# Two transformer layers on one core: wide score passes, narrower maxima, and normalisations, splits and last quantisation steps on GpSimd

## The reference

```python
xn = layernorm(x)
# layer 0, attention A, 16 heads of 8: cosine scores
W = (1 - arccos(clip(l2norm(q) @ l2norm(k).T, -0.999, 0.999)) / pi) ** 16
attn = (W / (W.sum() + eps)) @ v @ Wo.T + bo
# layer 0, "ffn": softmax attention (16 heads of 8) + 8 experts, top 2 of a softmax gate
ffn = softmax(q2 @ k2.T / sqrt(8)) @ v2 + sum_e(gate_e * (xn @ We + be))
x = x + attn + ffn
xn = layernorm(x)
# layer 1: causal attention with one head of 128, and a gated mlp of width 352 whose
# inputs and weights are rounded to FP4 in blocks of 16 (scale = block maximum / 6)
x = x + softmax(mask(q @ k.T)) @ v @ w_out.T + fp4lin(silu(fp4lin(xn, wg)) * fp4lin(xn, wu), wd)
```

## Time and profile before

| | before |
|---|---|
| median of 3 runs | 2050.38 us (2048.84 to 2050.67) |
| the profiled execution, its span | 2050.03 us, 2048.2 us |
| mean granted clock of TensorE | 0.924 |
| ACT busy | 1875.9 us, 92% |
| DVE busy | 1790.3 us, 87% |
| PE busy | 1625.1 us, 79% |
| POOL busy | 1062.5 us, 52% |

### The profile page before, as it was taken

How to read it: one execution, slowest core, us unless ns; L and a number is a source line. 1 busy time by engine, 2 the same in 40 slices (tenths; PEclk the granted TensorE clock), 3 DMA queues, 4 the chain that set the end, 5 groups by cost and what they waited for, 6 DMA issues and landing times.

```text
span 2048.2 us, 39684 instructions
## 1 busy us (share of the span) xinstructions
PE 1625.1 (79%) x12405; PEld 796.0 (39%) x12405; DVE 1790.3 (87%) x4071; ACT 1875.9 (92%) x2144; POOL 1062.5 (52%) x448
## 2 busy tenths in 40 slices
...
GB/s 41 4 4 1 6 6 0 5 6 5 6 5 6 0 5 6 5 6 5 6 0 5 6 5 6 5 6 0 5 6 5 6 5 6 0 5 7 4 4 6
DMA packets 21059, 11.21 MB, mean 5 GB/s; under 512 B 1431, under 2 KB 20953, under 8 KB 20956
## 3 DMA queue, kind: packets, MB, share of 16 engines
...
...
## 4 chain that ended last, share of the span: by engine, by line
ACT 40%; DVE 23%; issue 22%; PE 13%; POOL 1%; DVEq 1%; ACTq 1%; SPq 0%; DMA 0%; POOLq 0%
ACT curve L532 21%; ACT root L532 7%; ACT prob L532 3%; PE psM L1167 3%; DVE nmax L858 3%; DVE curve L848 3%; PE psM L1004 2%; ACT L563 2%; ACT L636 1%; PE psV L1199 1%; DVE h L421 1%; ACT hqT L532 1%; POOL qk L514 1%; PE psM L1151 1%; DVE hqT L417 1%
## 5 line engine op out<-in xcount | busy, mean ns | idle before, releaser
L532 ACT ACTIVATE curve<-curve 128x2048 f32<-128x2048 f32 x384 | 717.7, 1902 | 4.8 <-POOL curve L503 3.4
L500 POOL TENSOR_TENSOR root<-curve 128x2048 f32<-128x2048 f32 x128 | 460.1, 3600 | 426.1 <-DVE curve L852 425.9
L532 ACT ACTIVATE root<-root 128x2048 f32<-128x2048 f32 x256 | 484.4, 1905 | 8.1 <-POOL root L500 7.8
L503 POOL TENSOR_TENSOR curve<-curve,root 128x2048 f32<-128x2048 f32 x64 | 348.8, 5452 | 93.3 <-ACT root L532 93.3
L852 DVE TENSOR_SCALAR curve<-psS 128x1024 f32<-128x1024 f32 x256 | 306.0, 1216 | 25.3 <-PE psS L1035 19.1
L858 DVE TENSOR_REDUCE nmax<-psS 128x4 f32<-128x1024 f32 x256 | 308.8, 1214 | 7.2 <-PE psS L1044 6.9
L1199 PE MATMUL psV<-prob,vf 128*32 128x256 f32 x2048 | 270.8, 425 | 3.9 <-ACT prob L532 0.6
L532 ACT ACTIVATE prob<-psS 128x1024 f32<-128x1024 f32 x256 | 261.3, 1021 | 11.8 <-PE psS L1065 11.0
L1199 PE MATMUL psV<-curve,vc 128*32 128x256 f32 x2048 | 225.4, 408 | 40.0 <-ACT curve L532 36.3
L520 POOL TENSOR_TENSOR stk<-qk,stk 128x512 f16<-128x512 f32 x128 | 168.4, 1325 | 155.3 <-ACT stk L532 155.3
L848 DVE TENSOR_TENSOR curve<-curve,root 128x2048 f32<-128x2048 f32 x64 | 177.7, 2777 | 5.6 <-ACT root L532 5.6
...
## 6 DMA issues: line engine op xcount, KB each, us to landing
...
```

The lines of the kernel that those rows point to most:

```text
L500: nc.gpsimd.tensor_tensor(root[:, two], curve[:, p, two], curve[:, p, two], ALU.mult).then_inc(s_sq, 1)
L503: nc.gpsimd.tensor_tensor(curve[:, p, two], curve[:, p, two], root[:, two], ALU.mult).then_inc(s_half[0], 1)
L532: return nc.scalar.activation(out, in_, func, **kw)
```

## The change

- ACT: `arctan`, `wln` and `wexp` are two passes of 4096 columns each, in place of four of 2048. `norm`'s square and the four `high` copies go to POOL.
- POOL: it also does both normalisations (`xnT`, `xn1T`) and the last step (8) of both quantisations. `carry` is a one-column addition in front of some of these.
- Maxima: four heads' parts now stand in one group of 32 columns, so two transposes and a 256-column copy do for `maxT`. In `e`, a matrix pickb of ones and zeros takes the place of ones; its shape is the same. Two small setup instructions on VectorE build it.
- PSUM: psV is one bank for both attentions, so `pvw` waits for `oF` and `pvf` for `oC`; the misc banks are three.
- SCHEDULE is another order, with some other lags (`stack 2, 3`, `residual` 0 instead of 1, `pvf 7`, `oF`, `finf` 0 instead of -1, `p1T`, `s1e`, `rs1` -2 instead of -1, `quanth 0` -1 instead of -2, `m 4..6` 1 instead of 0).

```diff
+MISC_BANKS = 3
 SCHEDULE = [
...
+    ("table", 0, -1), ("stack", 2, 0), ("wln", 0, -1), ("wexp", 0, -1), ("c", 1, 0), ("quanth", 1, -2),
+    ("experts", 0, 0), ("stack", 3, 0), ("residual", 0, 0), ("c", 2, 0), ("wln", 1, -1), ("ln0", 0, 1), ("sq", 0, 0),
+    ("c", 3, 0), ("s1e", 0, -2), ("wexp", 1, -1), ("rstd0", 0, 1), ("pvw", 0, -1), ("experts", 1, 0), ("pvw", 1, -1),
+    ("m", 7, 0), ("quanth", 2, -2), ("fadd", 0, -1), ("pvw", 2, -1), ("pvw", 3, -1), ("ln", 0, 0), ("c", 4, 0),
+    ("p1T", 0, -2), ("xnT", 0, 1), ("pvw", 4, -1), ("pvw", 5, -1), ("quanth", 3, -2), ("sq", 1, 0), ("pvw", 6, -1),
+    ("maxT", 0, 0), ("quanth", 4, -2), ("quanth", 5, -2), ("sq", 2, 0), ("ln", 1, 0), ("c", 5, 0), ("pvw", 7, -1),
+    ("proj", 0, 1), ("c", 6, 0), ("proj", 1, 1), ("gmax", 0, 1), ("oC", 0, -1), ("e", 0, 0), ("o1", 0, -2),
+    ("e", 1, 0), ("norm", 0, 1), ("guess", 0, 1), ("rs1", 0, -2), ("finc", 0, -1), ("quanth", 6, -2), ("high", 0, 1),
+    ("e", 2, 0), ("c", 7, 0), ("choose", 0, 1), ("ln", 2, 0), ("pvf", 0, 0), ("e", 3, 0), ("w1", 0, -2),
+    ("pvf", 1, 0), ("high", 1, 1), ("ocT", 0, -1), ("gexp", 0, 1), ("e", 4, 0), ("stack", 0, 1), ("choose", 1, 1),
+    ("wo", 0, -1), ("e", 5, 0), ("newton", 0, 1), ("stack", 1, 1), ("load", 0, 1), ("pvf", 2, 0), ("ln1", 0, -1),
+    ("sq", 3, 0), ("ln", 3, 0), ("quanth", 7, -2), ("rstd1", 0, -1), ("e", 6, 0), ("stackT", 0, 1), ("quantx", 0, -1),
+    ("stackT", 1, 1), ("e", 7, 0), ("pvf", 3, 0), ("choose", 2, 1), ("quantx", 1, -1), ("unit", 0, 1),
+    ("quantx", 2, -1), ("quantx", 3, -1), ("table", 1, 0), ("pvf", 4, 0), ("quantx", 4, -1), ("xn1T", 0, -1),
+    ("choose", 3, 1), ("quantx", 5, -1), ("quantx", 6, -1), ("choose", 4, 1), ("quanth", 8, -2), ("pvf", 5, 0),
+    ("quantx", 7, -1), ("sigm", 0, 0), ("hT", 0, -2), ("p1", 0, -1), ("m", 0, 1), ("m", 1, 1), ("s1", 0, -1),
+    ("sigm", 1, 0), ("high", 2, 1), ("quantx", 8, -1), ("mul", 0, 0), ("xqT", 0, -1), ("mul", 1, 0), ("hmul", 0, -1),
+    ("hT", 1, -2), ("m", 2, 1), ("hmul", 1, -1), ("sigm", 2, 0), ("gu", 0, -1), ("pvf", 6, 0), ("pvf", 7, 0),
+    ("mul", 2, 0), ("sigm", 3, 0), ("oF", 0, 0), ("gu", 1, -1), ("mul", 3, 0), ("m", 3, 1), ("m", 4, 1), ("m", 5, 1),
+    ("stackT", 2, 1), ("stackT", 3, 1), ("finf", 0, 0), ("m", 6, 1), ("high", 3, 1), ("c", 0, 1), ("choose", 5, 1),
+    ("arctan", 0, 0), ("arctan", 1, 0), ("down", 0, -2), ("quanth", 0, -1),
 ]
...
-        psV = psum("psV", [P, 2, 2, T])
+        psV = psum("psV", [P, 2, T])
...
+            def carry(k):
+                nc.gpsimd.tensor_tensor(holdp[:, k:k + 1], iota8[:, 0:1], iota8[:, 0:1], ALU.add)
+            def normalise(src, means, rstd_, dst, s_newton, s_done, b):
+                pool.wait_ge(s_newton, due(s_newton, b))
+                carry(4 if dst is xn else 5)
+                for j in range(NT):
+                    nc.gpsimd.tensor_scalar(dst[:, j, :], src[:, j, :], means[:, j, 0:1], rstd_[:, j:j + 1],
+                                            ALU.subtract, ALU.mult).then_inc(s_done, 1)
...
+                if stage == "norm":
+                    pool.wait_ge(s_nsum, due(s_nsum, b - 1))
+                    pool.wait_ge(s_qkc, due(s_qkc, b))
+                    cos = qk[:, 0:2, :, :, :].rearrange("p k j h d -> p (k j h) d")
+                    nc.gpsimd.tensor_tensor(qsq[:, :, :], cos, cos, ALU.mult).then_inc(s_qsq, 1)
+                if stage == "high":
...
+                    pool.wait_ge(s_stkTp, due(s_stkTp, b - 1, arg + 1))
+                    carry(kind)
+                    nc.gpsimd.tensor_copy(hi, src).then_inc(s_stk1, 1)
...
                 if stage == "arctan":
-                    act.wait_ge(*half_done(b, arg))
-                    activate(two, two, ACT.Arctan).then_inc(s_atan, 1)
+                    act.wait_ge(*half_done(b, 2 * arg))
+                    act.wait_ge(*half_done(b, 2 * arg + 1))
+                    activate(four, four, ACT.Arctan).then_inc(s_atan, 1)
...
-                    cols = mstk[:, :, :, :].rearrange("p j (g h) c -> p j g (h c)", g=4)
-                    for g in range(4):
-                        for j in range(NT):
-                            ins = transpose(bankb[k][:, g, j * P:(j + 1) * P], cols[:, j, g, :], identb[:, :])
+                    cols = mstk[:, :, :, :].rearrange("p j h c -> p j (h c)")
+                    for j in range(NT):
+                        ins = transpose(bankb[k][:, 0, j * P:(j + 1) * P], cols[:, j, :], identb[:, :])
```

More of the change, by code:

```diff
@@ L53 @@
 SCHEDULE = [
[L54 to L73, removed]
@@ L237, in build @@
         psS = psum("psS", [P, 2, 2, 2, T])
[L238 to L239 removed]
+        psV = psum("psV", [P, 2, T])
+        psM = [psum(f"psM{k}", [P, 512]) for k in range(MISC_BANKS)]
         bank16 = [p[:, :].bitcast(F16).rearrange("p (g t) -> p g t", g=4) for p in psM]
@@ L350, in bank_read @@
         def bank_read(stage, arg, use, t, uses=MISC):
-            n = uses.index((stage, arg, use))
-            ring = [k for k in range(len(uses)) if k % 2 == n % 2]
+            n, banks = uses.index((stage, arg, use)), 2 if uses is SCORES else MISC_BANKS
+            ring = [k for k in range(len(uses)) if k % banks == n % banks]
             at = ring.index(n)
@@ L520, in run @@
                     nc.gpsimd.tensor_tensor(lo, src, hi, ALU.subtract).then_inc(s_stk, 1)
+                if stage == "quantx" and arg == FP4_STEPS - 1:
+                    fp4(pool, xn1[:, :, :].rearrange("p j d -> p (j d)"), xq1[:, :, :].rearrange("p j d -> p (j d)"),
+                        (qxa, qxr, qxe), s_qx, b, arg)
+                if stage == "quanth" and arg == FP4_STEPS - 1:
+                    fp4(pool, h[:, :, :].rearrange("p j n -> p (j n)"), h[:, :, :].rearrange("p j n -> p (j n)"),
+                        (qa, qr, qe), s_qh, b, arg)
                 if stage == "fadd":
```

102 lines of the change are left out of this document (49 added, 53 removed).

## The result

The changed kernel takes 2107.36 us (median of 4 runs, 2106.64 to 2111.15), the one before 2050.32 beside it: ratio 1.0283, 95% interval 1.0266 to 1.0301. It is 2.8% slower. The forecast was 2012 us, with 1950 to 2085 as its range; the time lies outside, on the side of rival B.

What follows compares the result with a forecast made beforehand. ScalarE, busy 97.6%, was taken as the bound. The six terms summed to a new step P of 58.6 us (before: 59.8); 195.7 us + 31 x P gave 2012 us, range 1950 to 2085.

Steps and rivals of the forecast that it cites:

- 5, ScalarE to `gexp`: ScalarE runs e 2, ln 2, e 3, ocT and gexp while VectorE stands at choose 0: 4.1 us.
- rival B: VectorE meets a fuller GpSimd, at mul 3 and newton: slower, step 60.6 us or 62.2; chance 0.27, C included.
- term 2: VectorE from hmul 1 to the end of c 5: old 25.4 us, waits removed, new work added, 28.6 us.
- term 1: ScalarE from ln1 to gu 1's sigmoid, 15.6 us, plus 1.0 us waiting for gu 1 on TensorE.
- term 6: VectorE's choose 0 and 1, w1, wo, ln1's moments and newton, which ScalarE's ln1 waits for: 3.1 us.
- terms 3 and 4: GpSimd's sq 2, then norm's square, 4.8 us; VectorE's sum and floor of norms and ScalarE's guess, 1.45 us.
- my loop: One round of waits through ScalarE, VectorE and GpSimd that sets the new step: 58.6 us.
- A row and a rule: VectorE and GpSimd share an SBUF port pair, held per instruction; meeting a sq could cost VectorE up to 3.6 us.
- Rival A: ScalarE stays the bound, the orders hide the rest: step 55.9 to 57.7 us, 1929 to 1984 us; chance 0.20.
- C: GpSimd's unmeasured copies and tensor_scalar cost near their upper ends; VectorE waits at quantx 0: 1.2 to 2.5 us, chance within B's.

Runs made afterwards that it cites:

- d4: Changed kernel with GpSimd's four sq and two mul on 32 of 2048 columns, the rest left undone: 2036 us, step 59.78 us.
- b2: Kernel before with only the narrow maxima (two transposes, 256-column copy, pickb): 2054.58 us, ratio 1.0025.
- d1: Changed kernel with only the second normalisation (xn1) back on VectorE: 2115.73 us, ratio 1.0343.
- c2: Changed kernel with mul 3 moved behind m 3 in SCHEDULE: 2106 us.
- a2: Changed kernel with ocT and gexp moved ahead of ln 2: 2107 us.
- a3: Changed kernel with norm's square back on ScalarE and norm moved right behind proj 1: 2138 us.
- c3: Changed kernel with mul 3 moved behind m 3, quanth 3 behind maxT and newton behind ln1: median 2110.84 us, ratio 1.0317.

## Why the prediction was wrong

My six terms, as I forecast them, in after and in d4 (ends and starts on VectorE's and ScalarE's timelines of one step). Each term ends where the next begins, so that they add up to the step whatever sets it; what the table shows is where the time lies:

| term | forecast | after | d4 |
|---|---|---|---|
| 1, `ln1` to `gu 1`'s sigmoid, with its wait | 16.6 | 16.9 | 17.2 |
| 2, `hmul 1` to `c 5` on VectorE | 28.6 | 31.1 | 29.2 |
| 3 and 4, square, norms, guess | 6.25 | 6.5 | 6.45 |
| 5, ScalarE to `gexp` | 4.1 | 4.1 | 4.1 |
| 6, `choose 0` to `ln1`'s moments | 3.1 | 3.46 | 2.8 |
| P | 58.6 | 62.05 | 59.8 |

**What failed: term 2.** Of the 3.45 us between forecast and measurement, 2.5 lie in this term, 0.3 in term 1, 0.25 in 3 and 4 and 0.36 in term 6 (there it is `newton`'s meeting). In it `mul 3` took 3.52 us where I put 2.7 (0.8), and `quanth 3` 1.47 where I carried over 0.88 (0.6): both are meetings, with `mul 2` and with `sq 1`. The rest is waits of VectorE: 0.71 us for ScalarE's rstd at 1007.35, and 0.61 for `finf`'s sums at 1057.93. The sums stand on TensorE behind the transposes of `stack 3`, which GpSimd ends at 1055.44, behind the lengthened `mul 2` and `carry`. I had taken the old stretch and struck its waits off, and the new order has its own. In d4, 1.9 of the 2.5 us are gone with GpSimd's long instructions.

**Right by luck: terms 3 and 4.** 6.25 forecast and 6.5 measured look like a path that was right, but `sq 2`, 3.6 us of the sum, does not set this stretch. In d4 it takes 0.24 us, and from the end of `c 5` (1017.15 in after, 1046.03 in d4) to the start of `guess` it is 5.95 and 5.97 us. After, then d4:

```profile
1017.22 3.60 POOL L521 TENSOR_TENSOR root<-curve 128x2048 f32<-128x2048 f32 x1 [3.94 <-DVE curve L875]
```

```profile
1022.18 1.02 ACT L574 ACTIVATE prob<-psS 128x1024 f32<-128x1024 f32 x1
1023.10 0.25 ACT L574 ACTIVATE lnn<-n 128x64 f32<-128x64 f32 x1
```

```profile
1046.12 0.24 POOL L523 TENSOR_TENSOR root<-curve 128x32 f32<-128x32 f32 x1 [6.95 <-DVE curve L878]
```

```profile
1052.00 0.25 ACT L577 ACTIVATE lnn<-n 128x64 f32<-128x64 f32 x1
```

`guess` waits for nothing in both (in after the sums of squares are ready at 1022.77): up to it ScalarE is in `e 1`, which stands on TensorE behind `proj` and `e 0`. That way isn't in my sum. The end of term 1 is no firm joint either: in after the sigmoid of `gu 1` is done at 1047.91, and VectorE is in `m 2` until 1048.19. So several ways of nearly the same length run side by side, and my loop was one of them.

**The meetings in the sum.** "A row and a rule" had the mechanism, and rival B its places: `mul 3` at 0.7 us (measured 0.8 over my 2.7), `newton` at 0.65 to 1.3 us (measured 0.60). B's P of 60.6 was short by what I hadn't found, `quanth 3`, and by the waits. I left the cost out of the sum although my own rows and a rule that they bear out both asked for it, on the ground that `sq` was not lengthened before; that says that an order can avoid meetings, not that this one does.

**ScalarE as the bound.** Wrong already for the kernel before, by b2: P 59.82 with 0.7 us less work on it. I counted every us off ScalarE as a gain to be lost elsewhere; b2 shows one place where a gain never was. Rival A fell with the result: ScalarE is busy 88%, not 97%.

**What held.** A pass of 4096 columns is 3.61 us (forecast 3.60), the copy of the maxima 0.383 (0.387), the square 1.04 (1.0), step 8 1.39 and 0.62 (1.5 and 0.7). ScalarE works 54.8 us a step (529.80 x 62.03 / 600; forecast 54.5). Of C's unseen operations, the copies are 0.61 us, under my 1.0, and the tensor_scalar of 128 columns 0.79, where I took 0.3 and had 1.0 as the other end. C's sign and its wait came with that: VectorE stood 1.23 us at `quantx 0` (1034.83) for the normalisation, but d1, where the wait is gone, is no shorter. `carry` is 0.53 us in the mean, where I took 0.1, because some meet VectorE. GpSimd comes to 44.3 us a step (forecast 42). The fill and the drain, which I left alone, became 11 us shorter. VectorE's saving of 2.7 us is not to be seen: it works 55.1 us a step (533.06 x 62.03 / 600) against 55.2 (553.29 x 59.82 / 600; the 54.7 of the prediction was misread). What left it came back as longer instructions, `newton` 0.6 us and L809 0.5 a step among them. The upper end of my range, P = 60.9, was called the first case of B, which is 60.6.

**What stays open.** d4, without GpSimd's long work, is only as fast as before. Whether an order of the changed kernel without meetings is much under 59.8 no run shows. Why one shortened link doesn't shorten the round I argue from c2, a2, a3 and d4: ways of equal length lie beside each other, and an order that avoids one meeting brings another. That it is so for every link is not shown. What the new order, the shared psV bank and the third misc bank do by themselves was not run. c3's spread of 32 us between runs of one program is not explained.
